# Branch convolution: the last two rows of a block are kept on chip by ACT copies, and eight rows are read for ten

## Chip, cores and metric

The kernel runs on one core of a Trainium2 chip. The metric is the device time of one execution in microseconds.

## What is computed

Layer 0 normalises x (4 x 192 x 128 x 128), makes 576 channels per pixel with a pointwise and a 3x3 depthwise convolution, and uses them twice: for channel attention, and for the branch convolution, the part that this case changes. Layer 1 is a bidirectional scan over pixels. Cut to the branch:

```python
qkv = jnp.einsum('bchw,oc->bohw', x, qkv_w[:, :, 0, 0, 0])
qkv = _conv3d(qkv[:, :, None], qkv_dw_w, groups=3 * c, pad=1)[:, :, 0]
f_all = qkv.reshape(b, hw, 3 * heads, cpg).transpose(0, 2, 1, 3)
f9 = jnp.einsum('bgnc,og->bonc', f_all, fc_w[:, :, 0, 0, 0]) + fc_b[None, :, None, None]
f_conv = f9.transpose(0, 3, 1, 2).reshape(b, 9 * cpg, h, w)
out_conv = _conv3d(f_conv[:, :, None], dep_w, groups=cpg, pad=1)[:, :, 0] + dep_b[None, :, None, None]
...
return out + out_conv
```

The 1x1 mixing (fc_w) and the 3x3 convolution (dep_w) over rows and columns are folded into one weight tile, wc.

## The kernel before

The kernel is a chain of stages with a barrier between them: gs (statistics), pw (pointwise), dw (depthwise, writes d), gr (gram), bc (`branch_conv`), aw, ap, and wb and wf twice. Tile names carry the stage as a prefix. Stage bc spans from about 2891 to 3904 us.

d holds, for each image b, padded rows of 128 pixels x 576 values; 576 values are 12 groups (G3) of 48 channels (CPG). A block i is eight output rows (ROUT), 16 blocks (NB) in all; it needs ten input rows. The loop takes four images in a block as two halves h of two images. For each image:

- SP's and POOL's queues load it into xp slot b % 2. The partition is `S * quad + pixel in a run of 32`, the free axes are four runs k, 32 slots s and 48 channels. A slot holds one (row, group) pair; 10 x 12 = 120 pairs are 30 slots in each of four quads of 32 partitions. SP loads quads 0 and 1, POOL quads 2 and 3, six DMAs each (NL = 6). A load waits for `turned`, the transposes of the image that had the slot. A (row, group) pair of 128 pixels x 48 channels is 24.6 KB. The two spare slots of a quad hold ones and flags for the biases and the image's edges.
- DVE (L881) turns 32 x 32 blocks, xp to z, so that the partition becomes (row, group) and the free axes are channel, image and pixel: four instructions an image, k = 0 to 3. They wait for both queues' loads of that slot, and for PE's products of the block before (`product`), since z[h] has one copy.
- PE (L842) multiplies z[:, h, c] by wc[:, c, dx] (128 rows by 32 columns), three shifts dx for each of four channels c4, into one of six PSUM banks; 12 such steps q a half.
- ACT (L820) evicts each bank into xt, and after 12 steps issues the store of t, 1536 KB (L823). PE waits for evictions through `added`.
- After the second half's transposes DVE does five ranking instructions of `order(i)` (L897 to L906) for the attention.

POOL builds mask and the ones before the loop, and DVE builds wc with them (L862 to L871). Engines run their own code in the order written, so what is issued behind a waiting instruction waits too.

Of the kernel before, what the change touches and what calls it, by code (L numbers as in the profile page):

```python
# [13 lines left out]

# [11 lines left out]
HEADS, CPG = 4, 48  # L26
# [666 lines left out]
def branch_conv(nc, d, fcb, branch_w, branch_b, attn_d, rank_d, t):  # L693


    RIN, ROUT = 10, 8
    Q, S = 30, 32
    FLAG, TOP, LOW = Q, Q + 1, S + Q
# [7 lines left out]
    with Stage(nc, "bc") as st:  # L706
# [3 lines left out]
        mask = st.sb("mask", [128, 3, ROUT])  # L710
        wc = st.sb("wc", [128, CPG, 3, JJ, ROUT])
# [12 lines left out]
        wl, consts, spread, rprod, rmade, flagged, tied, al, cmp, rank_stored = map(  # L724
            st.sem, ("wl", "consts", "spread", "rprod", "rmade", "flagged", "tied", "al", "cmp", "rank_stored"))
        p_loaded = [st.sem(f"p_loaded{h}") for h in range(2)]
        u_loaded = [st.sem(f"u_loaded{h}") for h in range(2)]
        stored = [st.sem(f"stored{h}") for h in range(2)]
        product, added, turned, passed = map(st.sem, ("product", "added", "turned", "passed"))
        block = st.block()  # L730
        NL = 6

        def load(queue, i, b, quads):
            for quad in quads:
                    for part in range(3):
                        lo = Q * quad
                        r = lo // G3 + part
                        first, last = max(lo, r * G3), min(lo + Q, (r + 1) * G3)
                        row = d[b, bass.ds((ROUT * i + r) * ROW, ROW)].rearrange("(k w n) -> w k n", k=NW, w=S)
                        c0 = (first - r * G3) * CPG  # L740
                        queue.dma_start(xp[S * quad:S * quad + S, b % 2, :, first - lo:last - lo, :].rearrange("p k s c -> p k (s c)"),
                                     row[:, :, c0:c0 + (last - first) * CPG]).then_inc((p_loaded if quads[0] == 0 else u_loaded)[b % 2], 16)

        def loads(queue, quads):
            for h in range(2):
                load(queue, 0, h, quads)
            for b in range(2):
                queue.wait_ge(turned, b + 1)
                load(queue, 0, b + 2, quads)
            with queue.Fori(0, NB - 1) as i:  # L750
                for b in range(B):
                    queue.wait_ge(turned, B * i + b + 3)
                    own_wait(queue, passed)
                    load(queue, i + 1, b, quads)

        @block.sync
        def _(sp):
            sp.wait_ge(consts, 2)
            dv = branch_w.rearrange("c o d y x -> o c (d y x)")
            sp.dma_start(taps[0:9, :, :], dv[:, :, 9:18]).then_inc(wl, 16)  # L760
            sp.dma_start(taps[9:10, :, 4:5], branch_b.rearrange("(a c k) -> a c k", a=1, k=1),
                         allow_slow_non_contiguous=True).then_inc(wl, 16)
            sp.dma_start(fcr[0:9, :], fcb).then_inc(wl, 16)
            sp.dma_start(a[:, :, :], attn_d.rearrange("(g p) k -> p g k", p=128)).then_inc(al, 16)
            loads(sp, (0, 1))
            sp.wait_ge(cmp, 5 * NB + 1)
            sp.dma_start(rank_d.rearrange("(g p) k -> p g k", p=128), rank[:, :, :]).then_inc(rank_stored, 16)
            sp.wait_ge(rank_stored, 16)
            for h in range(2):
                sp.wait_ge(stored[h], 16 * NB)  # L770

        @block.gpsimd
        def _(pool):
            nc.gpsimd.memset(taps, 0.0).then_inc(consts, 1)
            nc.gpsimd.memset(fcr[:, 0:G3], 0.0)
            nc.gpsimd.memset(fcr[:, G3:G3 + 1], 1.0).then_inc(consts, 1)
            nc.gpsimd.memset(mask[:, :, :], 1.0)
            nc.gpsimd.memset(tri[:, :, :], 1.0).then_inc(tied, 1)
            nc.gpsimd.memset(xp[:, :, :, Q:S, :], 0.0).then_inc(consts, 1)
            pool.wait_ge(consts, 3)  # L780
            nc.gpsimd.memset(xp[0:S, :, :, Q:Q + 1, :], 1.0).then_inc(consts, 1)
            pool.wait_ge(consts, 4)
            nc.gpsimd.memset(xp[S:2 * S, :, :, Q:Q + 1, :], 1.0).then_inc(consts, 1)
            pool.wait_ge(consts, 5)

            pool.wait_ge(tied, 1)
            nc.gpsimd.affine_select(out=tri[:, :, :], in_=tri[:, :, :], compare_op=ALU.is_gt, fill=0.0, base=0,
                                    pattern=[[1, CPG], [-1, CPG]], channel_multiplier=0).then_inc(tied, 1)
            for q in range(4):
                part = mask[S * q:S * q + S, :, :]  # L790
                nc.gpsimd.affine_select(out=part, in_=part, compare_op=ALU.is_ge, fill=0.0, base=Q * q,
                                        pattern=[[-G3, 3], [-G3, ROUT]], channel_multiplier=1).then_inc(consts, 1)
                pool.wait_ge(consts, 6 + 3 * q)
                nc.gpsimd.affine_select(out=part, in_=part, compare_op=ALU.is_ge, fill=0.0, base=G3 - 1 - Q * q,
                                        pattern=[[G3, 3], [G3, ROUT]], channel_multiplier=-1).then_inc(consts, 1)
                pool.wait_ge(consts, 7 + 3 * q)
                nc.gpsimd.affine_select(out=part, in_=part, compare_op=ALU.is_ge, fill=0.0, base=Q - 1,
                                        pattern=[[0, 3], [0, ROUT]], channel_multiplier=-1).then_inc(consts, 1)
                pool.wait_ge(consts, 8 + 3 * q)

            nc.gpsimd.affine_select(out=mask[:, :, :], in_=mask[:, :, :], compare_op=ALU.not_equal, fill=1.0, base=-FLAG,
                                    pattern=[[0, 3], [0, ROUT]], channel_multiplier=1).then_inc(consts, 1)
            pool.wait_ge(consts, 18)
            for n, (row, dy, rout, fill) in enumerate(((FLAG, 0, 0, 0.0), (FLAG, 2, ROUT - 1, 0.0),
                                                       (TOP, 0, 0, 1.0), (LOW, 2, ROUT - 1, 1.0))):
                nc.gpsimd.affine_select(out=mask[:, :, :], in_=mask[:, :, :], compare_op=ALU.not_equal, fill=fill,
                                        base=-row - 1000 * dy - 10000 * rout,
                                        pattern=[[1000, 3], [10000, ROUT]], channel_multiplier=1).then_inc(consts, 1)
                pool.wait_ge(consts, 19 + n)
            loads(pool, (2, 3))  # L810

        @block.scalar
        def _(act):
            act.sem_inc(added, NBANK)
            with act.Fori(0, NB) as i:
# [33 lines left out]
        def _(dve):  # L849
# [4 lines left out]
            for q in range(4):  # L854
                at = Q * q % G3
                last = nc.vector.tensor_copy(fcx[:, S * q:S * q + Q], ext[:, :, :].rearrange("p a g -> p (a g)")[:, at:at + Q])
            last.then_inc(spread, 1)
            for p, n in ((FLAG, 2), (LOW, 1)):
                last = nc.vector.tensor_copy(fcx[:, p:p + n], fcr[:, G3:G3 + 1].to_broadcast([10, n]))
            last.then_inc(spread, 3)  # L860
            dve.wait_ge(consts, 22)
# [23 lines left out]
            def flags(rows, value):  # L885
                for k in range(2):
                    last = nc.vector.memset(xp[rows, k, :, Q + 1 if rows.start == 0 else Q:S if rows.start == 0 else Q + 1, :], value)
                return last
# [20 lines left out]
            dve.wait_ge(tied, 2)  # L909
            dve.wait_ge(al, 16)  # L910
            turn(0, 0)
            turn(0, 1)
            dve.wait_ge(turned, B)
            flags(slice(0, S), 1.0).then_inc(flagged, 1)
            dve.wait_ge(flagged, 1)

            def body(i):
                for h in range(2):
                    dve.wait_ge(product, 2 * CQ * i + CQ * (h + 1))
                    turn(i + 1, h)  # L920
                order(i)
            with dve.Fori(0, NB - 2) as i:
                body(i)
            dve.wait_ge(turned, B * (NB - 1))
            flags(slice(S, 2 * S), 0.0).then_inc(flagged, 1)
            dve.wait_ge(flagged, 2)
            body(NB - 2)
# [916 lines left out]
```

## Time and profile before

| | |
|---|---|
| three runs, us | 7195.49, 7194.46, 7199.81 (median 7195.49) |
| profiled execution, us | 7192.32 |
| its span, us | 7190.7 |
| mean granted TensorE clock | 0.874 |
| busy: PE, DVE, ACT, POOL | 76%, 77%, 39%, 5% of the span |
| L881 transposes, busy | 711.3 us in 256 |
| L842 products, busy | 574.3 us in 9216 |
| L820 evictions, busy | 147.4 us in 384 |

Busy time is what an engine worked. Idle time of an engine costs something only where the chain that ends last runs through it, so the waits of a stage are to be read beside the busy time. A DMA queue is named by a number: q1 is SP's, q10 ACT's, q0 POOL's. The share of a queue is the time of its packets over 16 DMA engines.

### The profile page before, as it was taken

To read this page: it belongs to the slowest core of one execution; us is meant where nothing else is said; L and a number is where in the kernel's file an instruction comes from. 1 tells how busy PE (TensorE), PEld (TensorE's weight loads), DVE (VectorE), ACT (ScalarE), POOL (GpSimd) and SP (SyncE) were. 2 spreads that over 40 slices of the span, in tenths; PEclk is the share of its full clock that TensorE was granted. 3 is DMA by queue.
4 is the path that set the end of the run, shared out by engine and by line. 5 is a ranking of instruction groups with operands and counts; after the bars stand their busy time and mean duration, and the time that the engine had idled before them with its cause. 6 is when DMAs were issued, how large, how long until landed. Compare 5 with 4: busy or idle time off the path is not lost. (4 is left out here: it accounts for less than half of the span.)

```text
span 7190.7 us, 80281 instructions
## 1 busy us (share of the span) xinstructions
PE 5477.3 (76%) x24890; PEld 2259.0 (31%) x24890; DVE 5516.6 (77%) x4405; ACT 2783.6 (39%) x3511; POOL 349.1 (5%) x553
## 2 busy tenths in 40 slices
PE   0999999799999567356555777767759986775988
PEld 0333333333333367233332222222212222221222
DVE  6333333899999787788886666679979997997998
ACT  0222222111111477111111000036659994566998
POOL 0100100000000000222221000000000000000000
PEclk9999999899999778677777778778879998887999
DMA  8565564999999998799997999945557764555775
GB/s 301 177 199 182 189 196 159 265 275 267 279 270 270 234 234 212 178 252 253 249 248 183 253 267 269 268 157 202 200 179 250 245 210 157 193 196 198 241 252 182
DMA packets 1189809, 1615.51 MB, mean 225 GB/s; under 512 B 85252, under 2 KB 905157, under 8 KB 1159877
## 3 DMA queue, kind: packets, MB, share of 16 engines
q1 hardware_dynamic: 847301, 1314.23, 60.9%
q10 hardware_dynamic: 314880, 201.39, 10.0%
q0 software_dynamic: 27520, 98.54, 5.3%
q8 instruction: 57, 0.93, 0.1%
q14 instruction: 51, 0.42, 0.0%
HBM read 1006.55 MB, written 607.33 MB: 224 GB/s over the span
## 5 line engine op out<-in xcount | busy, mean ns | idle before, releaser
L508 PE MATMUL dw_p<-dw_it,dw_tt 128*128 128x512 f32 x2304 | 1026.5, 607 | 120.9 <-DVE dw_tt L424 83.1
L547 DVE SCALAR_TENSOR_TENSOR dw_vo<-dw_vi,keep_wv,dw_vo 128x2048 f32<-128x2048 f32 x384 | 903.1, 2352 | 13.6
L842 PE MATMUL bc_p<-bc_z,bc_wc 128*32 128x256 f32 x9216 | 574.3, 415 | 395.2 <-DVE bc_z L881 395.2
L320 PE MATMUL pw_p<-pw_xh,pw_wlo 128*112 128x512 f32 x1536 | 693.7, 601 | 186.3 <-POOL pw_xh L274 186.3
L881 DVE STREAM_TRANSPOSE bc_z<-bc_xp 128x1536 f32<-128x1536 f32 x256 | 711.3, 2847 | 151.9 <-DMA bc_xp<-d 151.4
L1090 PE MATMUL ap_p<-ap_vt,ap_pw 96*96 96x512 f32 x1024 | 594.0, 746 | 178.1 <-DMA ap_xt<-in_x 175.1
L508 PEld LDWEIGHTS dw_p<-dw_it,dw_tt 128*128 128x128 f32 x2304 | 442.1, 193 | 705.4 <-issue 673.1
L525 ACT ACTIVATE dw_ot<-dw_p 128x512 f32<-128x512 f32 x384 | 215.9, 599 | 931.3 <-PE dw_p L508 683.7
L375 DVE COPY pw_ut<-pw_p 112x512 f32<-112x512 f32 x384 | 247.3, 686 | 379.5 <-PE pw_p L326 377.4
L842 PEld LDWEIGHTS bc_p<-bc_z,bc_wc 128*32 128x32 f32 x9216 | 319.2, 119 | 650.4 <-issue 485.1
L820 ACT ACTIVATE bc_xt<-bc_p 128x256 f32<-128x256 f32 x384 | 147.4, 384 | 871.5 <-PE bc_p L842 871.5
L320 PEld LDWEIGHTS pw_p<-pw_xh,pw_wlo 128*112 128x112 f32 x1536 | 262.0, 177 | 610.4 <-issue 536.3
L1445 DVE TENSOR_TENSOR_SCAN wb_sums<-wb_ewt,wb_fb 128x3078 f32<-128x3078 f32 x64 | 424.3, 6630 | 2.3
L1728 DVE TENSOR_TENSOR_SCAN wf_sums<-wf_ewt,wf_fb 128x3078 f32<-128x3078 f32 x64 | 424.3, 6630 | 2.3
L664 DVE TENSOR_REDUCE gr_ss<-gr_sq 128x24 f32<-128x3072 f32 x64 | 315.8, 4992 | 118.1 <-ACT gr_sq L648 117.8
L1123 DVE TENSOR_TENSOR ap_xo<-ap_p,ap_tt 96x512 f32<-96x512 f32 x256 | 173.7, 686 | 283.4 <-PE ap_p L1090 183.9
L1090 PEld LDWEIGHTS ap_p<-ap_vt,ap_pw 96*96 96x96 f32 x1024 | 203.3, 205 | 568.6 <-issue 524.7
L625 PE MATMUL gr_p<-gr_qk 128*48 128x48 f32 x4096 | 286.6, 335 | 119.4 <-DMA gr_qk<-d 82.6
L648 ACT ACTIVATE gr_sq<-gr_qk 128x3072 f32<-128x3072 f32 x64 | 314.4, 5003 | 152.0 <-DMA gr_qk<-d 120.1
L326 PE MATMUL pw_p<-pw_xh,pw_whi 64*112 64x512 f32 x1536 | 362.5, 604 | 0.0
L1398 ACT ACTIVATE wb_fb<-wb_bb,wb_fac 128x1024 f32<-128x1024 f32 x192 | 206.8, 1141 | 365.4 <-DVE wb_bb L1454 365.4
L625 PEld LDWEIGHTS gr_p<-gr_qk 128*48 128x48 f32 x4096 | 284.4, 237 | 123.4 <-issue 114.9
(316 smaller groups left out, 8483.5 us busy)
## 6 DMA issues: line engine op xcount, KB each, us to landing
u<-pw_ut SPq DMA_DIRECT2D x64, 2240.0 KB, 12.7
dw_it<-u SPq DMA_DIRECT2D x192, 512.0 KB, 10.9
d<-dw_ot ACTq DMA_DIRECT2D x192, 512.0 KB, 12.1
gr_qk<-d SPq DMA_DIRECT2D x128, 768.0 KB, 9.1
bb_d<-wb_bb SPq DMA_DIRECT2D x64, 1536.0 KB, 5.1
wf_bb<-bb_d SPq DMA_DIRECT2D x64, 1536.0 KB, 7.8
bc_xp<-d SPq DMA_DIRECT2D x256, 288.0 KB, 12.0
bc_xp<-d POOLq DMA_DIRECT2D x256, 288.0 KB, 9.8
```

The costliest lines, as they stand in the source:

```text
L320: mm(pt[m % NBANK][e][:, :], wlo[:, wm], xh[:, h, 2 * e, cols], start=True, stop=False, skip_group_check=True)
L326: last = mm(pt[m % NBANK][e][:, :], whi[p, wm], xh[p, h, 1, cols], start=False, stop=True, skip_group_check=True)
L508: mm = nc.tensor.matmul(po[c][:, :].rearrange("p (b w) -> p b w", b=B), tt[:, h, 3 * c + dx, 0:H], it[:, h, B * c:B * (c + 1), dx:dx + W], ...
L547: nc.vector.scalar_tensor_tensor(vo[:, h], src, w, vo[:, h], ALU.mult, ALU.add).then_inc(tapped, 1)
L625: mm = nc.tensor.matmul(pg[h][p:p + CPG, :], qk[:, h, 0:CPG, w], qk[:, h, CPG:QK, w], start=w < 2, stop=w >= W - 2, skip_group_check=True)
L648: nc.scalar.activation(sq[:, e % 2, :, :].rearrange("p c w -> p (c w)"), qk[:, h, E * e:E * e + E, :].rearrange("p c w -> p (c w)"), ACT.S ...
L664: nc.vector.tensor_reduce(ss[:, n % 2, E * e:E * e + E], sq[:, e % 2, :, :], AX.X, ALU.add).then_inc(reduced, 1)
L842: mm = nc.tensor.matmul(po[q % NBANK][32 * c4:32 * c4 + 32, :, :], wc[:, c, dx, :, :].rearrange("p j r -> p (j r)"), z[:, h, c, :, dx:dx + ...
L881: last = nc.vector.transpose(z[:, h, :, b % 2, 1 + S * k:1 + S * k + S], xp[:, b % 2, k, :, :].rearrange("p s c -> p c s"))
L1090: mm = nc.tensor.matmul(po[2 * q + m][:, :], pw[:, b, k, m * HALF:(m + 1) * HALF], vt[:, b % 2, k, q * SUB:(q + 1) * SUB], start=k == 0, s ...
L1445: nc.vector.tensor_tensor_scan(row(sums[:, :, :, :])[:, ::-1], row(ewt[:, :, :, :])[:, ::-1], row(fb[:, g])[:, ::-1], ewt[:, 2, 1, CH:CH + ...
L1728: nc.vector.tensor_tensor_scan(row(sums[:, :, :, :]), row(ewt[:, :, :, :]), row(fb[:, g]), ewt[:, 0, 0, 0:1], ALU.mult, ALU.add).then_inc( ...
```

## The change

In blocks 2 to 14 the first two of the ten rows are not read. They are rows 8 and 9 of the block before, which stand in z at partitions 64 to 87 (HALO); ACT copies them to 96 to 119 (OLD) of z with `keep`, in two pairs of copies a half, one pair behind the sixth eviction and one behind the twelfth. DVE turns only partitions 0 to 95 then and waits for `copied`. Blocks 0, 1 and 15 read all ten rows: SP's queue loads the two old ones with EDGE_PIECES, and DVE turns 128 partitions. The pieces are cut anew: five DMAs for SP, all to quads 0 and 1, and five for POOL, three to quad 2 and two to quad 1. Quads 0 and 1 hold 32 pairs each and quad 2 holds 32, quad 3 the 24 old ones and the ones and flags. The mask is built otherwise, in as many steps, with one memset of xp for partitions 96 to 127.

```diff
-        NL = 6
+        NL = 5
+        SP_PIECES = ((0, 0, 2, 0, G3), (1, 0, 4, 8, 4), (0, G3, 3, 0, G3), (1, 4, 5, 0, G3), (0, 2 * G3, 4, 0, 8))
+        POOL_PIECES = ((2, 0, 8, 0, G3), (1, 4 + G3, 6, 0, G3), (2, G3, 9, 0, G3), (1, 4 + 2 * G3, 7, 0, 4), (2, 2 * G3, 7, 4, 8))
+        EDGE_PIECES = ((3, 0, 0, 0, G3), (3, G3, 1, 0, G3))
+
+        def load(queue, i, b, pieces, sem):
+            for quad, slot, r, g0, n in pieces:
+                row = d[b, bass.ds((ROUT * i + r) * ROW, ROW)].rearrange("(k w n) -> w k n", k=NW, w=S)
+                queue.dma_start(xp[S * quad:S * quad + S, b % 2, :, slot:slot + n, :].rearrange("p k s c -> p k (s c)"),
+                                row[:, :, g0 * CPG:(g0 + n) * CPG]).then_inc(sem[b % 2], 16)
...
+                        queue.wait_ge(turned, B * i + b - 1)
+                        own_wait(queue, passed)
+                    load(queue, i, b, pieces, sem)
+                    if edge and at_edge:
+                        load(queue, i, b, EDGE_PIECES, e_loaded)
...
+            block(0, True)
+            block(1, True)
+            with queue.Fori(2, NB - 1) as i:
+                block(i, False)
+            block(NB - 1, True)
...
-            nc.gpsimd.memset(xp[:, :, :, Q:S, :], 0.0).then_inc(consts, 1)
...
+            made(nc.gpsimd.memset(xp[OLD:128, :, :, NE:S, :], 0.0))
...
+            def keep(h, c0):
+                for b in range(2):
+                    last = nc.scalar.activation(z[OLD:OLD + NE, h, c0:c0 + CPG // 2, b, 1:1 + W],
+                                                z[HALO:HALO + NE, h, c0:c0 + CPG // 2, b, 1:1 + W], ACT.Copy)
+                last.then_inc(copied, 1)
...
+                        if keeps and q % (CQ // 2) == CQ // 2 - 1:
+                            keep(h, 4 * (q + 1) - CPG // 2)
...
+            evacuate(0, False)
+            with act.Fori(1, NB - 2) as i:
+                evacuate(i, True)
+            evacuate(NB - 2, False)
+            evacuate(NB - 1, False)
...
-            def turn(i, h):
+            def turn(i, h, edge):
+                rows = slice(0, 128 if edge else OLD)
...
+                    if edge:
+                        dve.wait_ge(e_loaded[b % 2], 32 * (2 * min(i, 2) + b // 2 + 1))
+                    else:
+                        dve.wait_ge(copied, 4 * i + 2 * h - 6)
...
-                    for k in range(NW):
-                        last = nc.vector.transpose(z[:, h, :, b % 2, 1 + S * k:1 + S * k + S],
-                                                   xp[:, b % 2, k, :, :].rearrange("p s c -> p c s"))
+                    for k in range(NW):
+                        last = nc.vector.transpose(z[rows, h, :, b % 2, 1 + S * k:1 + S * k + S],
+                                                   xp[rows, b % 2, k, :, :].rearrange("p s c -> p c s"))
```

On ACT, the end of the first half in the loop, from the sixth eviction on. Before, twelve evictions stand in a row and the store is behind them:

```order
162 L820 ACTIVATE bc_xt<-bc_p 128x256
163 L819 REGISTER_ALU
...
172 L820 ACTIVATE bc_xt<-bc_p 128x256
173 L819 REGISTER_ALU
174 L820 ACTIVATE bc_xt<-bc_p 128x256
175 L822 REGISTER_ALU
176 L823 ISA
177 L823 DMA t<-bc_xt 128x3072
```

and now:

```order
166 L840 ACTIVATE bc_xt<-bc_p 128x256
167 L831 ACTIVATE bc_z<-bc_z 24x24x128 x2
168 L839 REGISTER_ALU
169 L840 ACTIVATE bc_xt<-bc_p 128x256
...
179 L840 ACTIVATE bc_xt<-bc_p 128x256
180 L831 ACTIVATE bc_z<-bc_z 24x24x128 x2
181 L844 REGISTER_ALU
182 L845 ISA
183 L845 DMA t<-bc_xt 128x3072
```

Two pairs of copies have come in, the second of them ahead of the store. On POOL, an image's loads in the loop (partitions x runs x values); before:

```order
75 L741 DMA bc_xp<-d 32x4x576
76 L741 ISA
77 L741 DMA bc_xp<-d 32x4x576
78 L741 ISA
79 L741 DMA bc_xp<-d 32x4x288
80 L741 ISA
81 L741 DMA bc_xp<-d 32x4x288
82 L741 ISA
83 L741 DMA bc_xp<-d 32x4x576
84 L741 ISA
85 L741 DMA bc_xp<-d 32x4x576
```

and now:

```order
85 L747 DMA bc_xp<-d 32x4x576
86 L747 ISA
87 L747 DMA bc_xp<-d 32x4x576
88 L747 ISA
89 L747 DMA bc_xp<-d 32x4x576
90 L747 ISA
91 L747 DMA bc_xp<-d 32x4x192
92 L747 ISA
93 L747 DMA bc_xp<-d 32x4x384
```

One DMA is gone and 2304 values a run have taken the place of 2880; the second and the fourth of the five go to quad 1.

## Rows read from the trace of the kernel before

**Rows 1.** Windows of the stage: us, busy us (count) by engine, clock, DMA share, GB/s.

```profile
3668.00:3785.00 117.00, 71.92 (x1152) 39.60 (x1152) 96.22 (x42) 18.41 (x48) 24.66 (x45) 0.78 0.98 241
sum 703.00, PE 427.39 PEld 237.02 DVE 584.33 ACT 110.44 POOL 153.06; mean PE 71.23 PEld 39.50 DVE 97.39 ACT 18.41 POOL 25.51
```

**Rows 2.** Waits between 2890 and 3915: who, for whom, us, times, longest.

```profile
PE bc_p L842 <- DVE bc_z L881: 395.2, 32, 29.9
DVE bc_z L881 <- DMA bc_xp<-d: 151.4, 36, 8.9
```

**Rows 3.** Timeline of DVE: start, us, instruction, count, idle before and releaser.

```profile
3205.66 22.24 DVE L881 STREAM_TRANSPOSE bc_z<-bc_xp 128x1536 f32<-128x1536 f32 x8 [8.07 <-DMA bc_xp<-d]
...
3382.94 3.04 DVE L881 STREAM_TRANSPOSE bc_z<-bc_xp 128x1536 f32<-128x1536 f32 x1 [6.53 <-DMA bc_xp<-d]
...
3405.16 1.05 DVE L897 TENSOR_TENSOR bc_gt<-bc_a 128x864 f32<-128x864 f32 x1
...
3412.57 22.27 DVE L881 STREAM_TRANSPOSE bc_z<-bc_xp 128x1536 f32<-128x1536 f32 x8 [1.70 <-DMA bc_xp<-d]
3442.91 22.23 DVE L881 STREAM_TRANSPOSE bc_z<-bc_xp 128x1536 f32<-128x1536 f32 x8 [8.07 <-DMA bc_xp<-d]
...
3803.69 22.18 DVE L881 STREAM_TRANSPOSE bc_z<-bc_xp 128x1536 f32<-128x1536 f32 x8 [8.18 <-DMA bc_xp<-d]
```

**Rows 4.** Timeline of POOL from 3393 to 3412.

```profile
3395.53 3.66 POOL L741 DMA_DIRECT2D bc_xp<-d  x6 [14.76 <-DVE bc_z L881]
```

**Rows 5.** Timeline of ACT from 3405 to 3446.

```profile
3415.24 0.38 ACT L820 ACTIVATE bc_xt<-bc_p 128x256 f32<-128x256 f32 x1 [0.91 <-PE bc_p L842]
3416.54 0.38 ACT L820 ACTIVATE bc_xt<-bc_p 128x256 f32<-128x256 f32 x1 [0.92 <-PE bc_p L842]
...
3423.56 0.34 ACTq L823 DMA_DIRECT2D t<-bc_xt  x1
```

**Rows 6.** DMA queues from 3425 to 3428 (the store alone).

```profile
DMA packets 83, 1.02 MB, mean 340 GB/s; under 512 B 0, under 2 KB 0, under 8 KB 0
```

**Rows 7.** DMA queues from 3413 to 3420 (SP's q1, POOL's q0).

```profile
DMA packets 803, 1.86 MB, mean 266 GB/s; under 512 B 146, under 2 KB 387, under 8 KB 803
...
q0 software_dynamic: 368, 1.25, 68.0%
q1 hardware_dynamic: 435, 0.61, 36.3%
```

**Rows 8.** DMA queues, 2902 to 2909 (SP alone), then 2921 to 2926 (POOL alone).

```profile
DMA packets 805, 1.39 MB, mean 199 GB/s; under 512 B 94, under 2 KB 318, under 8 KB 804
...
DMA packets 278, 0.99 MB, mean 197 GB/s; under 512 B 64, under 2 KB 64, under 8 KB 278
```

**Rows 9.** DMA queues from 20 to 140, first stage.

```profile
DMA packets 2755, 40.13 MB, mean 334 GB/s; under 512 B 306, under 2 KB 306, under 8 KB 306
...
gs_xt<-in_x SPq DMA_DIRECT2D x19, 2048.0 KB, 7.2
```

**Rows 10.** Instructions of three ACT lines: ns min/median/max.

```profile
L1624 ACT ACTIVATE wf_rc<-wf_dn x64: 1474/1483/1497, 5326.5 to 7148.5; 128x1536 f32<-128x1536 f32 x64
L1651 ACT ACTIVATE wf_rs<-wf_lv x64: 629/630/635, 5350.5 to 7172.3; 128x512 f32<-128x512 f32 x64
L648 ACT ACTIVATE gr_sq<-gr_qk x64: 2750/3726/14342, 2455.9 to 2877.3; 128x3072 f32<-128x3072 f32 x64
```

**Rows 11.** Costliest groups of the page: busy, mean ns, idle before.

```profile
L648 ACT ACTIVATE gr_sq<-gr_qk 128x3072 f32<-128x3072 f32 x64 | 314.4, 5003 | 152.0 <-DMA gr_qk<-d 120.1
```

**Rows 12.** Instructions that transpose, 3082 to 3785: ns min/median/max.

```profile
L881 DVE STREAM_TRANSPOSE bc_z<-bc_xp x189: 2696/2761/3070, 3086.6 to 3784.9; 128x1536 f32<-128x1536 f32 x189
```

**Rows 13.** Timeline of POOL from 2890 to 2912.

```profile
2895.14 0.73 POOL L779 MEMSET bc_xp<- 128x768 f32 x1
2895.92 0.41 POOL L781 MEMSET bc_xp<- 32x384 f32 x1
```

**Rows 14.** Timeline of DVE from 2900 to 2910.

```profile
2905.24 3.90 DVE L862 MEMSET bc_wc<- 128x4608 f32 x1 [3.37 <-issue]
```

More of the change, by code:

```diff
@@ L15 @@
+import itertools
 import concourse.bass as bass
@@ L723, in branch_conv @@
         po = [st.ps(f"p{k}", [128, 2, W]) for k in range(NBANK)]
[L724 to L725 removed]
+        wl, consts, spread, rprod, rmade, flagged, al, cmp, rank_stored = map(
+            st.sem, ("wl", "consts", "spread", "rprod", "rmade", "flagged", "al", "cmp", "rank_stored"))
         p_loaded = [st.sem(f"p_loaded{h}") for h in range(2)]
+        e_loaded = [st.sem(f"e_loaded{h}") for h in range(2)]
@@ L727, in branch_conv @@
         u_loaded = [st.sem(f"u_loaded{h}") for h in range(2)]
         stored = [st.sem(f"stored{h}") for h in range(2)]
-        product, added, turned, passed = map(st.sem, ("product", "added", "turned", "passed"))
+        product, added, turned, copied, passed = map(st.sem, ("product", "added", "turned", "copied", "passed"))
         block = st.block()
-        NL = 6
[L733 to L750, printed above, removed]
-                for b in range(B):
-                    queue.wait_ge(turned, B * i + b + 3)
-                    own_wait(queue, passed)
-                    load(queue, i + 1, b, quads)
+        NL = 5
+        SP_PIECES = ((0, 0, 2, 0, G3), (1, 0, 4, 8, 4), (0, G3, 3, 0, G3), (1, 4, 5, 0, G3), (0, 2 * G3, 4, 0, 8))
@@ new lines, in loads, with block @@
+        def loads(queue, pieces, sem, edge, each=None):
+            def block(i, at_edge):
+                for b in range(B):
+                    if not (isinstance(i, int) and i == 0 and b < 2):
+                        queue.wait_ge(turned, B * i + b - 1)
[3 more added lines that the diff above has]
+                        load(queue, i, b, EDGE_PIECES, e_loaded)
+                if each:
+                    each(i)
+            block(0, True)
[3 more added lines that the diff above has]
+            block(NB - 1, True)
@@ L764, in _ @@
             sp.dma_start(a[:, :, :], attn_d.rearrange("(g p) k -> p g k", p=128)).then_inc(al, 16)
-            loads(sp, (0, 1))
+            loads(sp, SP_PIECES, p_loaded, True)
             sp.wait_ge(cmp, 5 * NB + 1)
@@ L784, in _ @@
[L784 to L809, printed above, removed]
@@ L810, in _, with made, where, rows @@
-            loads(pool, (2, 3))
+            count = itertools.count(3)
+            def made(op):
+                op.then_inc(consts, 1)
+                pool.wait_ge(consts, next(count))
+            def where(part, op, base, steps, channel, fill=0.0):
+                made(nc.gpsimd.affine_select(out=part, in_=part, compare_op=op, fill=fill, base=base,
+                                             pattern=[[steps[0], 3], [steps[1], ROUT]], channel_multiplier=channel))
+            def rows(part, base):
+                where(part, ALU.is_ge, base, (-G3, -G3), 1)
+                where(part, ALU.is_ge, G3 - 1 - base, (G3, G3), -1)
@@ new lines, in _ @@
+            made(nc.gpsimd.memset(mask[:, :, :], 1.0))
+            made(nc.gpsimd.memset(late[:, :, :], 1.0))
+            made(nc.gpsimd.memset(xp[OLD:128, :, :, NE:S, :], 0.0))
+            made(nc.gpsimd.memset(xp[OLD:128, :, :, NE:NE + 1, :], 1.0))
+            made(nc.gpsimd.memset(xp[OLD:128, :, :, NE + 2:NE + 3, :], 1.0))
+            made(nc.gpsimd.memset(tri[:, :, :], 1.0))
+            made(nc.gpsimd.affine_select(out=tri[:, :, :], in_=tri[:, :, :], compare_op=ALU.is_gt, fill=0.0, base=0,
+                                         pattern=[[1, CPG], [-1, CPG]], channel_multiplier=0))
@@ new lines, in _ @@
+            rows(mask[0:HALO, :, :], NE)
+            rows(mask[HALO:OLD, :, :], 4 * NE)
+            rows(mask[OLD:128, :, :], 0)
+            rows(late[HALO:OLD, :, :], HALO)
+            where(mask[HALO:OLD, :, :], ALU.is_ge, NE - 1, (0, 0), -1)
+            where(late[HALO:OLD, :, :], ALU.is_ge, -NE, (0, 0), 1)
+            where(mask[OLD:128, :, :], ALU.is_ge, NE - 1, (0, 0), -1)
+            made(nc.gpsimd.tensor_tensor(mask[HALO:OLD, :, :], mask[HALO:OLD, :, :], late[HALO:OLD, :, :], ALU.add))
@@ L812, in _ @@
+            where(mask[:, :, :], ALU.not_equal, -FLAG, (0, 0), 1, 1.0)
+            for row, dy, rout, fill in ((FLAG, 0, 0, 0.0), (FLAG, 2, ROUT - 1, 0.0), (TOP, 0, 0, 1.0), (LOW, 2, ROUT - 1, 1.0)):
+                where(mask[:, :, :], ALU.not_equal, -row - 1000 * dy - 10000 * rout, (1000, 10000), 1, fill)
+            loads(pool, POOL_PIECES, u_loaded, False)
         @block.scalar
@@ L814, in _, with evacuate @@
             act.sem_inc(added, NBANK)
-            with act.Fori(0, NB) as i:
+            def keep(h, c0):
[3 more added lines that the diff above has]
+                last.then_inc(copied, 1)
+            def evacuate(i, keeps):
                 for h in range(2):
@@ L853, in _ @@
             dve.wait_ge(spread, 2)
-            for q in range(4):
-                at = Q * q % G3
-                last = nc.vector.tensor_copy(fcx[:, S * q:S * q + Q], ext[:, :, :].rearrange("p a g -> p (a g)")[:, at:at + Q])
+            groups = ext[:, :, :].rearrange("p a g -> p (a g)")
+            for p, at, n in ((0, 0, 36), (36, 0, HALO - 36), (HALO, 0, NE), (HALO + NE, 4, S - NE), (OLD, 0, NE)):
+                last = nc.vector.tensor_copy(fcx[:, p:p + n], groups[:, at:at + n])
             last.then_inc(spread, 1)
[L858 to L861, printed above, removed]
+            nc.vector.tensor_copy(fcx[:, FLAG:FLAG + 3], fcr[:, G3:G3 + 1].to_broadcast([10, 3])).then_inc(spread, 3)
+            dve.wait_ge(consts, 2 + NCONST)
             nc.vector.memset(wc[:, :, :, :, :], 0.0).then_inc(rmade, 1)
@@ L908, in _, with body @@
             dve.sem_inc(cmp, 1)
-            dve.wait_ge(tied, 2)
             dve.wait_ge(al, 16)
-            turn(0, 0)
-            turn(0, 1)
+            turn(0, 0, True)
+            turn(0, 1, True)
             dve.wait_ge(turned, B)
-            flags(slice(0, S), 1.0).then_inc(flagged, 1)
+            flags(TOP, 1.0).then_inc(flagged, 1)
             dve.wait_ge(flagged, 1)
-            def body(i):
+            def body(i, edge):
                 for h in range(2):
                     dve.wait_ge(product, 2 * CQ * i + CQ * (h + 1))
-                    turn(i + 1, h)
+                    turn(i + 1, h, edge)
                 order(i)
[L922 to L925, printed above, removed]
+            body(0, True)
+            dve.wait_ge(turned, 2 * B)
+            flags(LOW, 0.0).then_inc(flagged, 1)
+            with dve.Fori(1, NB - 2) as i:
+                body(i, False)
             dve.wait_ge(flagged, 2)
-            body(NB - 2)
+            body(NB - 2, True)
             order(NB - 1)
```

20 lines of the change are left out of this document (9 added, 11 removed).

## Prediction

> **What bounds the kernel now.** I read the windows of the branch convolution's stage first [rows 1]. In six windows of 117 to 118 us each, DVE is busy for 584.3 of 703 us (83%), PE for 61%, ACT for 16%, and in the last of them the DMA engines for 0.98 of the time; PE's granted clock there is 0.78, a mean between its levels of 1.2 and 2.4 GHz. So DMA and DVE both come close to the whole time, and the question is which of them is waited for. The waits of the stage [rows 2] say: PE waits 395.2 us for DVE's transposes, DVE waits 151.4 us for loads into xp, and nobody in DVE's row waits for PE or ACT. The chain is load, transpose, and PE only follows.
>
> The timeline of DVE [rows 3] shows the beat. A half block (two images) is eight transposes in 22.2 to 22.3 us, 11.15 us an image. Starts stand at 3382.94, 3412.57 and 3442.91: 29.6 and 30.3 us apart. Over ten blocks, 3205.66 to 3803.69, a block takes 59.8 us. DVE waits at both starts: 8.07 us where no ranking work precedes, 1.70 us behind the five ranking instructions (3405.16 to 3410.87, 5.7 us with what lies between). It waits only at the first image of a pair, for the second is already there. That is the cycle of one xp slot: the slot is free when its image is turned, half way through the eight transposes (3394.1, 3423.7), and full again at 3412.57 and 3442.91, 18.5 and 19.2 us later. 11.15 + 18.8 = 29.9 us for a half. To shorten a block, these 18.8 us must shrink.
>
> What is in them? Before the first bytes lie about 2.0 us: POOL issues 1.4 us after the slot is free (3395.53) [rows 4], and a little is needed to land. The store of t, 1.57 MB, is issued almost when the slot is free (ACTq at 3423.56, freed 3423.7) [rows 5]; the window in which it flows alone shows 340 GB/s [rows 6], so 4.6 us. Then come the image's 2.95 MB (120 row-group tiles of 24.6 KB), half on SP's queue to partitions 0 to 63, half on POOL's to 64 to 127. A window where both flow has 266 GB/s, 1.25 MB of POOL against 0.61 MB of SP, that is 179 and 87 GB/s [rows 7]; either queue alone has 199 and 197 GB/s [rows 8]. So POOL's 1.475 MB takes 8.2 us, SP has moved 0.72 MB by then and needs 3.8 us alone for the rest: 12.1 us. 2.0 + 4.6 + 12.1 = 18.7, the measured wait. I trust the decomposition because it closes.
>
> **The change, part by part.** *Two rows less for 13 of 16 blocks* (2 to 14). An image has 96 tiles and not 120, 48 on each queue, 1.180 MB. But the split over partitions is another: 64 tiles go to partitions 0 to 63 (60 before), 32 to 64 to 95, and POOL now carries 16 of the lower ones. Where both queues write the lower half no row of before exists. Bounds: 266 GB/s, as if halves didn't matter, or 198 GB/s, what 32 partitions of one half took alone. I take 198, because the same queue with 128 partitions reached 334 GB/s in the first stage [rows 9], so the queue is not what holds it to 198, and the partitions are what differs (with the packet's length). With the shares of rows 7 (67% POOL's): POOL's 0.786 MB to the upper part at 179 takes 4.4 us (SP 0.38 MB), its 0.393 MB to the lower part at 133 takes 3.0 us (SP 0.19 MB), SP's remaining 0.61 MB alone 3.0 us. Sum 10.4 against 12.1: **1.67 us a half, 3.3 us a block, 43.4 us in 13 blocks**. A fifth of the bytes would have promised 2.4 us a half.
>
> The Trainium skill ("SBUF — State Buffer", section on the DMA port swizzle) says that partitions 0 to 63 reach only the same eight of 16 ports that 0 to 31 reach, and 64 to 127 the other eight. By that rule the new split is lopsided, two to one, and the sum stands as I made it; by a limit of each queue alone POOL would need 6.6 us, SP 3.1 more, 9.7 in all, 2.4 us a half and 62.7 us. The trace agrees with it as far as rows 8 and 9 go; two queues in one half no run here shows.
>
> *The ten-row blocks that stay* (0, 1, 15): SP carries the two old rows too, 72 tiles, 1.77 MB. Its lonely tail is then 1.19 MB, 6.0 us: 13.4 us, 1.3 us more than now. Blocks 1 and 15 have two halves each, block 0 one that is waited for: 5 x 1.3 = **6.6 us lost**.
>
> *ACT's copies*: in each half two pairs of 24 x 3072 elements, SBUF to SBUF. No such instruction is in the trace; the nearest are 1536 elements in 1.483 us and 512 in 0.630 us [rows 10], a slope of 0.833 ns an element, so 3072 take 2.76 us. The only one with 3072 elements, in the gram stage, has a least of 2.750 but a median of 3.726 and a mean of 5.003 us [rows 10, 11]. I take 2.76, for the stage of the copies disturbs DVE little (transposes from 2.70 to 3.07 us) [rows 12], and keep 5.0 as the upper bound. ACT then has 24 x 0.38 + 8 x 2.76 = 31 us of work in 59.8, 49 at 5.0. Queued behind the first pair are six evictions; PE has six PSUM banks and 1.3 us for each step [rows 5], 7.8 us, against 5.5 us of copies, so it isn't stopped. Queued behind the second pair are the store and the next half's evictions. The next transposes into z wait for it: copies end at 3423.5 + 5.5 = 3429.0, the transposes come at 3442.9 less 1.7. 12 us to spare; **cost nothing**. At 5.0 us the first pair runs from 3415.6 to 3425.6, six evictions of 0.38 to 3427.9, the second pair to 3437.9: still hidden, by 3 us.
>
> *The store, 5.5 us later*: it now comes while the loads run and not before them. Its bytes are the same, so I charge nothing, and keep as a bound that the free ride it has while POOL's queue starts up is lost.
>
> *Fewer partitions in the transposes* (96, not 128): the duration follows elements per partition in all rows I have; between nothing and a quarter of 11.15 us I take nothing.
>
> *POOL's constants*: one memset of 3072 elements takes the place of one of 768 (0.73 us); at the slope to 384 elements (0.41 us) [rows 13] it is 2.6 us. With the others equal in number (16 selects for 17, and one addition), DVE, which waits 3.37 us for them [rows 14], starts **2.1 us later**. The loads that SP and POOL issue before the loop are hidden behind the building of wc.
>
> Sum: -43.4 + 6.6 + 2.1 = -34.7 us. The profiled execution took 7192.32 us (span 7190.7), 3.2 under the median 7195.49; on the median: 7161 us.
>
> **The rivals.** *A, the store takes the gain back.* Now it flows when queues are empty anyway. In the middle of a load, an image's end is pushed out, the next image's POOL pieces are already in flow, and SP's tail meets them at 87 and not 198 GB/s. For it: SP's queue ends last in every wait. Against: the bytes in the wait fall all the same. If it eats 1.67 us a half, the time is 7195.5 + 8.7 = 7204. Chance 0.20, a fifth of that with a gain over the bound.
>
> *B, the lower half alone sets the load.* If the wait follows the tiles of partitions 0 to 63, it grows by 64/60 of 12.1 us, 0.8 us a half, 26 halves: +21, with 8.7: 7225 us, slower. It decides where POOL's lower pieces cost SP more than their bytes. Chance 0.10. The rule named above makes this likelier than the bytes alone would.
>
> *C, ACT becomes the bound.* 9.1 + 8c exceeds 59.8 us at c = 6.3 us a copy, 2.3 times my value and above the mean of rows 11. At 7 us a block takes 65.1, +69 us: 7270. Chance 0.06.
>
> *D, more than the sum.* DVE's own work is 2 x 22.3 + 5.7 = 50.3 us a block; if the wait fell under that (or the transposes got shorter), a block saved up to 9.5 us: 13 x 9.5 = 124, less 8.7: 7080. With queue limits only, 7141. Chance 0.19 together.
>
> **How the numbers follow.** My forecast has 0.45 with its own range 7140 to 7180. The range over cases reaches down into D and up over A: 7105 to 7208. What a measurement of this kernel can tell from no change is 0.2%, 14.4 us. Faster: 0.45 + 0.19 + 0.04 = 0.68; same: the rest of A, 0.16; slower: B and C, 0.16.
>
> **What would show it.** A block of 56 to 57 us between first transposes; the wait for loads 6.4 us at the starts without ranking (8.07 less 1.67) and near nothing behind the ranking; copies of 2.8 us; the store issued 5.5 us after PE's last product; transposes still 2.8 us. I am wrong if a window with both queues on the lower half keeps 266 GB/s, if the store stretches the wait, or if DVE is seen waiting for ACT.

## The result

| | median us | ratio to before, 95% interval |
|---|---|---|
| before, first series | 7194.95 | |
| after, first series (6 runs each) | 7138.35 | 0.9932 [0.9913, 0.9951] |
| after, measured again with a later series | 7150.99, before 7199.07 | 0.9920 [0.9903, 0.9937] |

The changed kernel is faster by 0.7 to 0.8%. The medians alone differ by 57 us in the first series and by 48 in the later one. 7161 was forecast, 35 us less than before; 7138 lies in the range of 7105 to 7208 and outside the forecast's own 7140 to 7180 by a hair, 7151 lies inside both.

Windows of the stage of the kernel after, columns as in [rows 1]:

```profile
3189.00:3299.00 110.00, 70.66 (x1168) 40.22 (x1164) 100.29 (x43) 60.69 (x64) 22.02 (x40) 0.81 0.82 228
...
sum 661.00, PE 424.16 PEld 238.76 DVE 601.18 ACT 363.74 POOL 132.09; mean PE 70.69 PEld 39.79 DVE 100.20 ACT 60.62 POOL 22.02
```

Two blocks now fit a window of 110 us where they needed 117 to 120. DVE's share has gone from 83 to 91%, ACT's from 16 to 55%, the DMA engines' has fallen from 0.98 to 0.82 (0.96 to 0.98 and 0.82 to 0.85 over all six windows). So the stage is no more one that DMA fills. Its waits, after, answer to [rows 2]:

```profile
PE bc_p L869 <- DVE bc_z L911: 350.9, 32, 29.9
DVE bc_z L911 <- DMA bc_xp<-d: 96.0, 22, 9.9
```

and DVE's timeline, after, to [rows 3]:

```profile
3244.05 22.61 DVE L911 STREAM_TRANSPOSE bc_z<-bc_xp 96x1536 f32<-96x1536 f32 x8 [4.32 <-DMA bc_xp<-d]
3266.48 1.12 DVE L927 TENSOR_TENSOR bc_gt<-bc_a 128x864 f32<-128x864 f32 x1
...
3271.21 1.05 DVE L936 TENSOR_REDUCE bc_rank<-bc_gt 128x864 f32 x1 [0.23 <-DVE bc_gt L933]
3272.18 22.45 DVE L911 STREAM_TRANSPOSE bc_z<-bc_xp 96x1536 f32<-96x1536 f32 x8
3298.93 5.95 DVE L911 STREAM_TRANSPOSE bc_z<-bc_xp 96x1536 f32<-96x1536 f32 x2 [4.31 <-DMA bc_xp<-d]
```

A block is 3298.93 - 3244.05 = 54.9 us here. The half that ends with the ranking is 28.1 us and the next transposes follow with no wait at all: that half is DVE's own work. The other is 26.8 us with 4.3 us of waiting. Its slot is free at 3272.18 + 11.2 = 3283.4 and full at 3298.93: 15.5 us, where it was 18.5 and 19.2 (medians of the 13 halves without ranking: 15.2, where it was 18.7). Ninety-six partitions are turned in the time of 128 (22.45 against 22.27 us for eight).

The loads have shrunk for the transposes of blocks 2 to 14. The 26 halves that end with a wait for such loads took 777.2 us before and 719.0 after, in the second profile of after 720.7: 58.2 and 56.5 us less, 2.2 us a half. The five halves that end with a wait for ten rows took 142.7 us before, 150.8 and 146.9 after: 8.1 and 4.2 us are given back. From POOL's first instruction to the first transposes it is 53.7 for 51.2 in both profiles.

I use "stage" below for the time from the first product's start to the last one's start; before and after (columns: min/median/max ns, first and last start):

```profile
L842 PE MATMUL bc_p<-bc_z,bc_wc x9216: 377/378/637, 2964.0 to 3903.2; 128*32 128x256 f32 x197
```

```profile
L869 PE MATMUL bc_p<-bc_z,bc_wc x9216: 377/378/637, 2954.6 to 3843.7; 128*32 128x256 f32 x197
```

939.2 and 889.1 us; the second profile of after has 888.1 (2965.1 to 3853.2). The stage is 50 us shorter (58.2 less 8.1), the size of the ratio. The two profiled executions differ by 59.7 us, and 11.9 of that lies ahead of the stage (POOL's first instruction at 2879.7, before 2891.6), where nothing was changed: single profiles move by that much, so the stage and the ratio are what I compare. A stage is read from one profiled execution. Where little should differ, it differs by 1 us (the two profiles of after), by 4 (after without its copies) and by 6 (before, and before with the copies alone): 8 us is near that, 20 is not.

### The profile page after: what moved, and what is told of

It reads as the page before. It is cut to its first block and busy times, and to the rows that moved or that the text cites. A ratio compares the mean times of both kernels' runs of the same rounds, so it can differ in the third digit from the quotient of the medians.

```text
span 7131.0 us, 79759 instructions
## 1 busy us (share of the span) xinstructions
PE 5462.3 (77%) x24890; PEld 2256.2 (32%) x24890; DVE 5513.8 (77%) x4405; ACT 3045.9 (43%) x3615; POOL 315.8 (4%) x490
## 5 line engine op out<-in xcount | busy, mean ns | idle before, releaser
L911 DVE STREAM_TRANSPOSE bc_z<-bc_xp 96x1536 f32<-96x1536 f32 (+1 forms) x256 | 718.5, 2911 | 96.1 <-DMA bc_xp<-d 96.0
## 6 DMA issues: line engine op xcount, KB each, us to landing
u<-pw_ut SPq DMA_DIRECT2D x64, 2240.0 KB, 12.7
```

The lines of the kernel that those rows point to most:

```text
L911: last = nc.vector.transpose(z[rows, h, :, b % 2, 1 + S * k:1 + S * k + S], xp[rows, b % 2, k, :, :].rearrange("p s c -> p c s"))
```

## The experiments

Ratios are to the kernel before on the same chip.

| run | stage, us | ratio to before, 95% interval |
|---|---|---|
| before | 939.2 | 1 |
| after | 889.1, 888.1 | 0.9932 [0.9913, 0.9951], 0.9920 [0.9903, 0.9937] |
| copies alone | 945.2 | 0.9994 [0.9983, 1.0006] |
| after without copies | 884.8 | 0.9922 [0.9908, 0.9936] |
| POOL's lower pieces to the upper half | 881.3 | 0.9932 [0.9916, 0.9947] |
| after, store late | 869.0 | 0.9923 [0.9907, 0.9938] |
| after, ranking cut in two | 876.8 | 0.9929 [0.9914, 0.9943] |
| after, copies doubled | 917.8 | 0.9964 [0.9949, 0.9979] |
| bytes alone | 861.3 | 0.9887 [0.9871, 0.9903] |
| ranking cut, old rows on POOL | 879.9 | 0.9925 [0.9911, 0.9938] |
| ranking cut and store late | 839.1 | 0.9867 [0.9846, 0.9888] |
| before, store late | 917.9 | 0.9968 [0.9952, 0.9985] |
| after, two stores a half | 870.6 | 0.9896 [0.9875, 0.9917] |

**Copies alone, in the kernel before.**

```diff
+            def keep(h, c0):
+                for b in range(2):
+                    part = z[64:88, h, c0:c0 + CPG // 2, b, 1:1 + W]
+                    last = nc.scalar.activation(part, part, ACT.Copy)
+                last.then_inc(copied, 1)
...
+                        if q % (CQ // 2) == CQ // 2 - 1:
+                            keep(h, 4 * (q + 1) - CPG // 2)
...
+                    wait(dve, copied, 4 * i + 2 * h - 2)
```

> The kernel before with ACT's copies alone (in place, partitions 64 to 87 of z, the same sizes and places, and DVE's wait for them); ten rows are still read. If the copies are hidden and the store of t is issued as soon as the evictions are done, as the trace of after shows it (issue beside the first copy of the second pair), the time is that of before, 7195 us within 10. If the copies push the store into the loads and stretch the slot's wait, it is slower by up to 1.7 us a half, 32 halves, 7250 us.

0.9994: nothing, as the first theory had it. The copies are hidden under 30 us halves.

**After without its copies.**

```diff
-                        if keeps and q % (CQ // 2) == CQ // 2 - 1:
-                            keep(h, 4 * (q + 1) - CPG // 2)
...
-                    else:
-                        dve.wait_ge(copied, 4 * i + 2 * h - 6)
```

> After without ACT's copies and without DVE's wait for them (the two old rows are stale, so the branch is left wrong in blocks 2 to 14). If ACT costs nothing: 7138 us within 10. If the copies do delay evictions, the store or the transposes, it is faster than after by what they cost; more than 10 us would show that ACT is in the chain.

0.9922 against 0.9932 and 0.9920: no difference that can be told. ACT costs nothing in the changed kernel either. The trace of after says where they lie (ACT, start, us):

```profile
3284.51 0.38 ACT L840 ACTIVATE bc_xt<-bc_p 128x256 f32<-128x256 f32 x1 [0.33 <-PE bc_p L869]
3284.92 2.79 ACT L831 ACTIVATE bc_z<-bc_z 24x3072 f32<-24x3072 f32 x1
3285.05 0.34 ACTq L845 DMA_DIRECT2D t<-bc_xt  x1
3287.61 2.77 ACT L831 ACTIVATE bc_z<-bc_z 24x3072 f32<-24x3072 f32 x1
```

The reader should see the third row. The store stands behind both copies in the program, and is issued 0.13 us after the first of them starts: its own wait is for the evictions, the queue's instruction does not wait for an engine that is still at work on what stands ahead. It is 0.13 us in all 20 halves of blocks 3 to 12, and the store's packets flow from 3287 on, before the second copy has ended at 3290.4. My "5.5 us later" never happened.

**POOL's lower pieces to the upper half.**

```diff
+        INNER = ((2, 0, 8, 0, G3), (3, 0, 6, 0, G3), (2, G3, 9, 0, G3), (3, G3, 7, 0, 4), (2, 2 * G3, 7, 4, 8))
...
-                    load(queue, i, b, pieces, sem)
+                    load(queue, i, b, pieces if edge or at_edge else INNER, sem)
```

> After, but in blocks 2 to 14 POOL writes its two lower pieces to partitions 96 to 127, where they are not read (quad 1's second half is stale in those blocks). Bytes and packets stay, the split over partitions becomes 48 to 48. If two queues in the lower half are held to 198 GB/s, as the prediction took it, a half that waits for loads gets 0.75 us shorter: 13 to 26 halves, 7118 to 7128 us. If the partitions make no difference while the bytes are equal: 7138 us within 7.

The ratio is that of after (0.9932), the stage 7 to 8 us shorter, near what stages differ by of themselves. The halves without ranking, which wait for loads, are 26.8 us here and 27.1 and 27.2 in after. That is the place of the 0.75 us that I had added for two queues in one half: at most 0.4 of it is there. A window of after in which SP's and POOL's queues load together, POOL's for the most part into the lower half, is slower than the 266 GB/s of [rows 7]:

```profile
DMA packets 323, 0.85 MB, mean 214 GB/s; under 512 B 45, under 2 KB 45, under 8 KB 323
```

That is 214 GB/s (3300 to 3304). But not all of the difference is the half's: the pieces are cut otherwise than before, with packets of 1536 and 3072 bytes beside those of 4608. Over 18 images of the second slot, which no store meets, the two queues moved 217 GB/s together in after while POOL's second piece was in flight (218 in the second profile), and 245 GB/s here, where the same piece goes to the upper half. So the lower half costs a tenth of the rate in that piece, and balancing the split hardly moves the wait.

**After, the store late.**

```diff
+                    if keeps:
+                        act.wait_ge(copied, 4 * i + 2 * h - 2)
                     act.dma_start(t[bass.ds(i, 1), h].rearrange("a p n -> (a p) n"),
```

> After, but the store of t waits until the half's copies are done, 5.5 us later than now, as the prediction supposed it to be. If a store in the middle of the loads takes its time from them one for one, the slot's wait grows by up to 1.7 us where DVE waits for loads, 13 halves, 7160 us. If it flows beside them at 400 GB/s in all, as in windows of after, nothing changes: 7138 us within 10.

By the stage neither: it is 20 us shorter than after's. The ratio, 0.9923, doesn't tell it from after alone. The half without ranking is 24.6 us here where after has 27.1; the one with it has become 29.4, with a wait of 1.3 us between its two images. This made me look at where the store lies. The rows are of ACT's queue (packets, MB, share of 16 engines) in one wait of the first slot, from free to full, in after (3338.8 to 3354.0) and here (3341.3 to 3354.0):

```profile
q10 hardware_dynamic: 144, 1.57, 26.0%
...
q10 hardware_dynamic: 42, 0.52, 10.5%
```

In after the whole store lies inside the wait that DVE pays for. Here its first packets come 11 us after the slot is free, when the loads are nearly done, and two thirds of its bytes have left the wait. In the median of the halves without ranking 0.60 of 1.57 MB are left in it, and the wait is 12.7 us for 15.2: 1 MB less at some 400 GB/s would be 2.4 us, by estimate. The rest of the store meets the second image's loads, for which DVE had not waited before.

**Ranking cut in two.**

```diff
                 for h in range(2):
                     dve.wait_ge(product, 2 * CQ * i + CQ * (h + 1))
                     turn(i + 1, h, edge)
-                order(i)
+                    order(i, h == 0, h == 1)
...
+                if not second:
+                    return
```

> After, with the five ranking instructions cut in two: two of them behind the first half's transposes, three behind the second's. In after a half behind the ranking is 28.1 us with no wait for loads (22.5 of transposes and 5.6 of ranking: DVE's own work), the other is 27.1 and waits 4.3 us. If that reading is right, both halves become bound by the loads, about 27 us: 1.1 us a block, 13 to 15 blocks, 14 to 17 us faster than after. If the loads only moved their wait from one half to the other (the two halves share a fixed 55 us), nothing changes.

Stage 876.8, 12 us less. In blocks 2 to 14 the halves are 26.0 to 28.6 us, 27.4 in the mean of either kind, and both kinds wait for loads, 0.7 to 2.6 us where three ranking instructions stand ahead and 2.2 to 3.9 where two do, so the first reading of the profile holds. The ratio, 0.9929, lies between the two of after, so by the whole kernel's time the gain is not shown.

**Copies doubled.**

```diff
             def keep(h, c0):
+                for b in range(2):
+                    part = z[0:NE, h, c0:c0 + CPG // 2, b, 1:1 + W]
+                    nc.scalar.activation(part, part, ACT.Copy)
```

> After, with as many copies again of partitions 0 to 23 in place: four of 2.79 us where two stood, as if a copy took 5.6 us. ACT's sum is then 9.1 + 16 x 2.79 = 54 us of a block of 55. By the prediction's slack (12 us behind the last product at 2.76 us a copy, 3 us at 5.0) the transposes begin to wait for ACT: at 5.6 us a copy the second pair ends some 1 to 3 us too late, 7150 to 7215 us. If the slack is larger, 7138 us within 10.

7178.44 us, as worked out: the slack of the prediction is about right. Waits of its stage:

```profile
DVE bc_z L914 <- ACT bc_z L834: 76.8, 14, 7.2
DVE bc_z L914 <- DMA bc_xp<-d: 45.7, 14, 6.8
```

DVE waits for ACT now. In after the last copy of a half ends at 3290.4 and the transposes that need it start at 3298.93, 8.5 us later and not 12, for the beat has become shorter. Doubling the copies adds 5.6 us behind PE's last product, and by estimate 3.4 more, because the first four copies (11.2 us) outlast PE's six steps (7.8 us). Rival C was a true one, at twice the price of a copy and not at 2.3 times.

**Bytes alone**, in the layout of before.

```diff
-        NL = 6
+        NL = 4
...
                         first, last = max(lo, r * G3), min(lo + Q, (r + 1) * G3)
+                        if last - first < G3 and not whole:
+                            continue
```

> The kernel before, with four DMAs of 288 KB a queue and image instead of four of 288 and two of 144 KB: each quad leaves out its six-slot piece after the first pair (those slots keep old rows, so the branch is wrong). 96 tiles an image as in after, but in the old layout, 48 to the lower and 48 to the upper half, no copies, 128 partitions turned, and no ten-row blocks. If fewer bytes alone give what after gives (wait of a slot from 18.8 to 15.5 us), a block takes 55 us from the start: 16 blocks x 4.5 = 70 us, 7125 us. If the bytes give the 1.67 us of the prediction and something of the new layout the rest: 7140 to 7145 us.

7115.77 us and 78 us less stage, more than the 70 expected. 28 halves are 27.4 us in the mean where before has 29.9: 2.5 us a half. The bytes alone, with 288 KB DMAs (eight an image for twelve), no copies and no new split, give all that after has and more. So nothing of the new layout helps. Of the 28 us between this stage and after's, 15 to 19 lie in the five halves where after still loads ten rows (132.2 us here, 150.8 and 146.9 in after) and 8 to 10 in the 26 others, 0.3 to 0.4 us a half.

**Ranking cut, the old rows of blocks 0, 1 and 15 on POOL's queue** (the label says late, but the store is where after has it).

```diff
-            loads(sp, SP_PIECES, p_loaded, True)
+            loads(sp, SP_PIECES, p_loaded, False)
...
-            loads(pool, POOL_PIECES, u_loaded, False)
+            loads(pool, POOL_PIECES, u_loaded, True)
```

> After with the ranking cut in two as in the run before and, further, the two old rows of blocks 0, 1 and 15 loaded by POOL's queue and not by SP's. In the prediction SP's lonely tail in the five halves of ten-row blocks costs 6.6 us. If that is right, POOL, which moves two bytes in three where both flow, takes them for less: 3 to 6 us faster than the split ranking alone. If the rows cost what they cost by their bytes, no difference between the two.

0.9925 against 0.9929, stage 879.9 against 876.8, the five halves with ten rows 145.8 us against 145.6: no difference. What the ten-row blocks cost is not SP's tail.

**Before, the store late** (and the copies, as a timer).

```diff
...
                     act.wait_ge(added, NBANK + 2 * CQ * i + CQ * (h + 1))
+                    act.wait_ge(copied, 4 * i + 2 * h + 2)
...
```

> The kernel before with in-place copies as in the run of the copies alone (945 us of stage), and the store waits for them. All ten rows are read. Theory now: a store that is issued ahead of a slot's loads holds them up for its own 4 to 5 us, one that meets them in flight runs beside them at some 400 GB/s in all; so a later store makes the kernel before faster too, 1 to 2 us a half, 32 to 60 us: stage 885 to 915. The rival: the bytes alone set the wait and a store costs its bytes wherever it lies: stage 940 to 950, no change.

Ten rows, all bytes, and the stage falls from 945.2 (copies alone) to 917.9 us. The ratio falls to 0.9968 from 0.9994; the two intervals touch (up to 0.9985 here, from 0.9983 there), so the stage shows it more surely than the whole time. The stage lies just above the theory's 885 to 915 and well below the rival's 940 to 950. By the halves it is less clear: the 26 halves of blocks 2 to 14 went from 779.6 to 760.0 us, 0.75 us a half, under the 1 to 2 that the theory asked. POOL and ACT of this run:

```profile
3260.76 3.66 POOL L741 DMA_DIRECT2D bc_xp<-d  x6 [15.62 <-DVE bc_z L891]
```

```profile
3265.64 0.34 ACTq L832 DMA_DIRECT2D t<-bc_xt  x1
```

The store follows the first load by 4.9 us. It is still inside the wait with all its bytes. ACT's queue in one wait of the first slot, with the copies alone (3361.0 to 3379.1) and here (3348.4 to 3366.1):

```profile
q10 hardware_dynamic: 144, 1.57, 25.9%
...
q10 hardware_dynamic: 144, 1.57, 21.6%
```

The same bytes take 25.9% of 18.1 us, 4.7 us of the 16 engines, where the store flows mostly by itself, and 21.6% of 17.7 us, 3.8 us, where it flows among loads. So the place alone is worth under 1 us a wait; the larger gain of the late store in after came with bytes that left the wait.

**After, two stores a half.**

```diff
-                    act.wait_ge(added, NBANK + 2 * CQ * i + CQ * (h + 1))
...
+                            act.wait_ge(added, NBANK + 2 * CQ * i + CQ * h + q + 1)
+                            half, n = q // (CQ // 2), CQ // 2 * 2 * W
+                            act.dma_start(t[bass.ds(i, 1), h].rearrange("a p n -> (a p) n")[:, n * half:n * half + n],
```

> After with the store of a half cut in two of 768 KB, the first behind the sixth eviction, some 9 us ahead of where the whole one is issued now, while DMA still loads the pair's second slot. By the theory of the place, the first part runs beside loads that nobody waits for, and the part that meets the waited slot is half as long: stage 870 to 880 against 889. If the two parts only take bandwidth at two places: 885 to 895.

870.6 us and 0.9896 beside after's 0.9920: the stage is as expected, the ratio's intervals overlap. Half of the store (0.79 MB in the median) lies in a wait of the first slot, which is 14.2 us for 15.2, a smaller gain than those bytes would give at 400 GB/s; why is open.

**Ranking cut and store late.** The edits of the ranking cut in two and of the late store in after, together.

> After with two edits together: the store waits for the half's copies (the run with the store late had 869 us between the first product and the last, after 889), and the ranking is cut in two (877 us). If each takes away its own wait, the stage comes to 857 us or less, 7115 to 7125 us. If both live off the same slack, it stays at 869: 7135 to 7140.

839.1 us, and 7104.81 us in all, 0.9867 [0.9846, 0.9888], clear of after (0.9920) in the same series. DVE in this run:

```profile
3254.96 22.69 DVE L913 STREAM_TRANSPOSE bc_z<-bc_xp 96x1536 f32<-96x1536 f32 x8
3277.44 1.15 DVE L930 TENSOR_TENSOR bc_gt<-bc_a 128x864 f32<-128x864 f32 x1
3278.37 1.18 DVE L931 TENSOR_TENSOR bc_eq<-bc_a 128x864 f32<-128x864 f32 x1
3279.34 11.67 DVE L913 STREAM_TRANSPOSE bc_z<-bc_xp 96x1536 f32<-96x1536 f32 x4
3291.89 11.18 DVE L913 STREAM_TRANSPOSE bc_z<-bc_xp 96x1536 f32<-96x1536 f32 x4 [0.88 <-DMA bc_xp<-d]
...
3306.31 5.85 DVE L913 STREAM_TRANSPOSE bc_z<-bc_xp 96x1536 f32<-96x1536 f32 x2
```

This block is 51.4 us with 0.9 us of waiting (52 us in the mean of blocks 2 to 14, with 0.9 to 1.9 us of waiting): DVE is nearly the bound, as rival D had it, but only once the store is out of the way and the ranking spread.

**The changed kernel again**, unedited, in the series of the three runs before this.

> The changed kernel once more, beside the three others on one chip: stage 889 us, ratio to before 0.993.

7150.99 us, 0.9920 [0.9903, 0.9937], and a stage of 888.1 us for 889.1: the first result holds, and the other runs of this series are read against it.

## Why the prediction was right, and where its sum was not

*Direction, mechanism and place: right.* The cycle of one xp slot was the bound, its wait shrank, and the copies are hidden (shown by two runs).

*The load term was too small*: 1.67 us a half, 43.4 in all. Measured: 2.2 us a half, 58.2 and 56.5 in all. The wait of a slot fell by 3.3 us and more (18.8 to 15.5; in the median 18.7 to 15.2). The halves without ranking used 3.0 us of it (30.1 to 27.1 in the mean), those with ranking only 1.4 (29.6 to 28.2), because DVE's own 28.1 us come up there. The sign that I had named, 6.4 us of wait where no ranking precedes, measured 4.5 and 4.7 in the medians of the two profiles. Two things were wrong in the term. First the price of both queues in the lower half, 0.75 us: by the run that moves POOL's pieces it is 0 to 0.4 us. The port rule of the Trainium skill ("SBUF — State Buffer", section on the DMA port swizzle) made me choose the lower bound of two; the trace agrees in direction (217 GB/s for 245 in one piece), the wait hardly shows it. Without it my own sum had 2.4 us of wait a half, 62.7 us in all and 7141, which came nearer.

Second, the store. I split the wait into 2.0 + 4.6 + 12.1 us as if the store always stood ahead of the loads, and trusted the split because it closed. It fits one of the two waits that I had read. In the kernel before, from 3424 to 3429, the store flows alone and both load queues stand still. In the other half, where it is issued at 3395.46 and POOL's first load at 3395.53, SP's loads come first and the store flows among loads of both queues; from 3397 to 3402 the kernel before has

```profile
DMA packets 348, 1.96 MB, mean 391 GB/s; under 512 B 23, under 2 KB 33, under 8 KB 235
...
q10 hardware_dynamic: 113, 1.39, 72.3%
```

That wait was 18.5 us and the first 19.2, so that the sum closed says little. In after the slot comes free earlier while the store hangs on PE: 3284.73 for POOL's first load, 3285.05 for the store. The window of after from 3288 to 3293, where all three queues flow, has

```profile
DMA packets 324, 2.02 MB, mean 404 GB/s; under 512 B 20, under 2 KB 20, under 8 KB 211
```

404 GB/s, against 266 with the loads alone [rows 7] and 340 for the store alone [rows 6]; 1.39 of the 2.02 MB are the store's. POOL's first packets come 5.1 to 5.9 us after the slot is free before (medians over blocks 3 to 12), and 2.5 us after it in after (2.5 to 3.5 in the second profile). A later store shortens the stage by 27 us with ten rows and by 20 with eight. Two effects are in that: its place among the loads, under 1 us a wait where no byte leaves the wait, and the bytes that leave the wait, 2.5 us for 1 MB in after with the store late. In the step from before to after all of the store stays in the wait, so of the two only the first can be at work; that it supplies the missing 0.8 us or so is argued from its size. Rival A had the store's move with the wrong sign and, as the ACT rows show, with a delay that doesn't occur.

*Ten-row blocks* 6.6 us: the five halves with ten rows cost 8.1 us in one profile and 4.2 in the other, right in size. The reason given, SP's tail, is not borne out: with the rows on POOL's queue nothing changed. So the size was luck, and what makes these halves longer stays open.

*POOL's constants* 2.1 us: 2.5 in both profiles, with the memset at 2.65 us for the 2.6 of the estimate. *Copies*: 2.789 us in the median for 2.76. *Fewer partitions*: nothing, as taken. *Rival B* fell: with 64 lower tiles for 60 the wait fell. *Rival C* holds, but begins earlier than at 6.3 us a copy: at 5.6 us DVE already waited for ACT, for the chain of copies behind PE's last product fills before ACT's sum does. I had worked out that chain for the copies' slack, with the longer beat of the kernel before, and then priced the rival by the sum. *Rival D* is half true: one half of each block is DVE's already.

## What to carry to other kernels

Where a slot is emptied and filled in turn, the bound is the wait of one slot and not the stage's mean DMA rate: read when it is free and when it is full, and count the bytes of every queue that flow in between, stores too. Taking a fifth of the loads' bytes shortened that wait by a sixth. A store that was held back until the slot was nearly full left 1 MB outside the wait, and the wait fell from 15.2 to 12.7 us; one that was held back but stayed inside gained less than 1 us. When a wait falls, look at once which engine's own work comes up next: here 5.6 us of ranking in one half of two. Spreading it over both was worth 12 us of the stage by itself and 30 on top of the late store.

## What was not expected of the hardware

A DMA that stands behind two copies on ACT is issued 0.13 us after the first of them starts, not 5.5 us later. Three queues together moved 404 and 391 GB/s where two loading queues moved 266 and the store alone 340. And the same store of 1.57 MB took 4.7 us of the DMA engines where it flowed mostly by itself and 3.8 us where it flowed among loads.
